# Gathered token rows staged through DRAM and turned on VectorE in the expert part of an attention and mixture-of-experts kernel

## The reference, cut to what matters

```
x = layernorm(x + attention(x))                  # 16 x 1024 tokens of 256 features
logits = x @ wr.T; idx = top 2 of 8 experts      # gate = softmax over the two
xg = x[dispatch]                                 # rows of each expert's tokens, at most 5120
h  = gelu(xg @ w1[e] + b1[e])                    # 256 -> 1024
y  = h @ w2[e] + b2[e]                           # 1024 -> 256
out = sum over the two experts of gate * y
x = layernorm(x + out)
```

## Time and profile before

| what | value |
|---|---|
| time of the runs | 2178.67 us median, 2173.41 to 2183.92 |
| span of the profiled execution, first to last instruction | 2074.6 us |
| the median less the span | 104.1 us |
| PE busy | 2003.8 us, 97% |
| DVE busy | 1457.5 us, 70% |
| ACT busy | 1230.1 us, 59% |
| POOL busy | 1249.4 us, 60% |
| mean granted TensorE clock | 0.990 of full speed |
| DMA moved | 173.30 MB, 84 GB/s |

### The profile page before, as it was taken

How to read it: one execution, slowest core, us unless ns; L and a number is a source line. 1 busy time by engine, 2 the same in 40 slices (tenths; PEclk the granted TensorE clock), 3 DMA queues, 4 the chain that set the end, 5 groups by cost and what they waited for, 6 DMA issues and landing times.

```text
span 2074.6 us, 51556 instructions
## 1 busy us (share of the span) xinstructions
PE 2003.8 (97%) x16208; PEld 1949.7 (94%) x16209; DVE 1457.5 (70%) x4361; ACT 1230.1 (59%) x2770; POOL 1249.4 (60%) x1321
## 2 busy tenths in 40 slices
PE   7999999999889999999999999999999999999996
PEld 6988888988879999999999999999999999999996
DVE  3787877878767686667668666766776676666665
ACT  3566666666645565655556566556565656565563
POOL 1277776776766655656556565556555565655564
PEclk9999999999989999999999999999999999999998
DMA  5244443442232121112112111131132122221221
GB/s 191 84 133 137 139 132 125 148 134 93 83 131 82 48 73 57 51 42 96 51 51 93 56 53 56 56 100 55 60 101 64 56 67 64 67 64 62 69 69 51
DMA packets 102242, 173.30 MB, mean 84 GB/s; under 512 B 26179, under 2 KB 70430, under 8 KB 102064
## 3 DMA queue, kind: packets, MB, share of 16 engines
q0 software_dynamic: 45104, 84.59, 13.4%
q1 hardware_dynamic: 57088, 88.18, 12.7%
HBM read 120.52 MB, written 68.97 MB: 91 GB/s over the span
## 4 chain that ended last, share of the span: by engine, by line
PE 57%; issue 5%; POOL 4%; DMA 4%; DVE 2%; ACT 1%; DVEq 1%; POOLq 0%; ACTq 0%; SPq 0%
PE y_ps L1732 29%; PE h_ps L1716 26%; DMA rows<-x_rows,pick_idx 3%; PE tb_ps L1696 2%; POOL slot_table L461 1%; POOL rows L1407 1%; DMA out<-y,put_idx 1%; POOL base L1420 1%; ACT h_ps L1531 0%; POOL rstd_b L1413 0%; POOL out L1431 0%; DVE y_raw L1578 0%; DVE y L1611 0%; DMA table_in<-slot_table 0%; DVE h_lo L1643 0%
## 5 line engine op out<-in xcount | busy, mean ns | idle before, releaser
L1531 ACT ACTIVATE h_ps<-h_ps,b_sb 128x256 f32<-128x256 f32 x1000 | 403.8, 445 | 566.7 <-PE h_ps L1716 566.7
L1732 PE MATMUL y_ps<-w_hi,h_hi 128*128 128x256 f32 x2000 | 568.1, 284 | 1.8 <-DVE h_lo L1643 1.8
L1716 PE MATMUL h_ps<-bt_hi,w_hi 128*128 128x256 f32 x2000 | 554.8, 277 | 3.0 <-DVE bt_lo L1560 1.5
L1732 PE MATMUL y_ps<-w_hi,h_lo 128*128 128x256 f32 x2000 | 557.0, 278 | 0.0
L1732 PE MATMUL y_ps<-w_lo,h_hi 128*128 128x256 f32 x2000 | 556.4, 278 | 0.0
L1716 PE MATMUL h_ps<-bt_lo,w_hi 128*128 128x256 f32 x2000 | 553.5, 277 | 0.0
L1716 PE MATMUL h_ps<-bt_hi,w_lo 128*128 128x256 f32 x2000 | 553.4, 277 | 0.0
L1716 PEld LDWEIGHTS h_ps<-bt_hi,w_hi 128*128 128x128 f32 x2000 | 376.3, 188 | 4.7 <-issue 2.7
L1732 PEld LDWEIGHTS y_ps<-w_hi,h_hi 128*128 128x128 f32 x2000 | 377.3, 189 | 3.3 <-DVE h_lo L1643 3.1
L1643 DVE TENSOR_TENSOR h_lo<-h_ps,h_hi 128x512 fp32r<-128x512 f32 x500 | 332.3, 682 | 64.1 <-ACT h_hi L1534 63.9
L1732 PEld LDWEIGHTS y_ps<-w_hi,h_lo 128*128 128x128 f32 x2000 | 376.5, 188 | 0.0
(11 more groups left out here) (281 smaller groups left out, 3615.6 us busy)
## 6 DMA issues: line engine op xcount, KB each, us to landing
xt_raw<-in_x_t SPq DMA_DIRECT2D x32, 512.0 KB
x_raw<-in_x SPq DMA_DIRECT2D x64, 256.0 KB, 3.3
w_raw<-in_w SPq DMA_DIRECT2D x16, 1024.0 KB
x_rows<-x_sb SPq DMA_DIRECT2D x32, 512.0 KB, 3.9
out<-alone SPq DMA_DIRECT2D x32, 512.0 KB, 4.5
slot_table<-entry,where POOLq DMA_INDIRECT x256
out<-y,put_idx POOLq DMA_INDIRECT x253
rows<-x_rows,pick_idx POOLq DMA_INDIRECT x250
```

The lines of the kernel that those rows point to most:

```text
L1531: nc.scalar.activation(half, half, ACT.Gelu_apprx_tanh, bias=b1_sb[:, bass.ds(e * FT + 2 * g + i, 1)]).then_inc(gelu_done, 1)
L1716: ins = nc.tensor.matmul(h_ps[:, g, (f % 2) * BLK:(f % 2 + 1) * BLK], w[:, c:c + P], v[:, k, :], start=(i == 0), stop=(i == 3 * DK - 1))
L1732: ins = nc.tensor.matmul(y_ps[:, t, :], v[:, g, h:h + P], w[:, c:c + D], start=(f == 0 and t == 0 and part == 0), stop=(f == FT - 1 and t ...
```

## The change

A block's rows no longer go from the gather to PE. SP stores the gathered tile to a DRAM buffer `stage` (`store_rows`) and loads it back in four DMAs (`load_x4`), one for each band of 64 features, so that each 32 partitions of `x4` hold one band of 32 tokens at a time. DVE turns the 32x32 pieces with one transpose (`turn_rows`, L1603 of the changed kernel) into the SBUF tile `turned`, from which ACT and DVE make `bt_hi` and `bt_lo`. Feature d then lies on partition d // 2, so the weights `w1` are loaded as "(p k) f", and the transposes that remain on PE (the first block and the four small ones) read every second feature. ACT's two copies go: SP loads `base` from `stage` (`load_base`). The gather runs one block further ahead, gather(n + 2) in body n; the tile `rows` is free again when its store has landed (`stored`), and `pick` moves to the head of DVE's body. Block 1's rows are gathered before the expert part begins, into `rows_second`. The loads of the next expert's weights and of `b2` move from SP to ACT.

```diff
+    stage_dram = nc.dram_tensor("stage", ((E * BLOCKS + 2) * BLK, D), F, kind="Internal").ap()
+        rows_second = keep("rows_second", [P, BT, D])
+        def interleaved(row, k):
+            return row.rearrange("p (i k) -> p k i", k=DK)[:, k, :]
             sp.dma_start(w_raw[:, 0:W1].rearrange("p (k f) -> p k f", k=DK),
-                         w1[e, :, :].rearrange("(k p) f -> p k f", p=P)).then_inc(w_loaded, 16)
+                         w1[e, :, :].rearrange("(p k) f -> p k f", p=P)).then_inc(w_loaded, 16)
...
-                for t in range(BT):
-                    pool.indirect_dma_start(
-                        out=rows[:, t, :], out_offset=None, in_=x1_dram,
-                        in_offset=bass.IndirectOffsetOnAxis(ap=table_in[:, t, 0:1], axis=0)).then_inc(gathered, 16)
+                for block, dst, landed in ((0, rows, first_gathered), (1, rows_second, gathered)):
+                    for t in range(BT):
+                        pool.indirect_dma_start(
+                            out=dst[:, t, :], out_offset=None, in_=x1_dram,
+                            in_offset=bass.IndirectOffsetOnAxis(ap=table_in[:, block * BT + t, 0:1], axis=0)).then_inc(landed, 16)
...
-            x1_next = sb("x1_next", [P, BT, D])
+            x4 = sb("x4", [P, BLK // 32, D // 4])
+            turned = sb("turned", [P, 2 * BLK])
...
+                def store_rows(n, src, done):
+                    sp.dma_start(block_of(n).rearrange("(t p) d -> p t d", p=P), src[:, :, :]).then_inc(done, 16)
+                def load_x4(n):
+                    sp.wait_ge(stored, 16 * n)
+                    by_band = block_of(n).rearrange("(g j) (c e) -> c j g e", j=32, c=4)
+                    for c in range(4):
+                        sp.dma_start(x4[c * 32:(c + 1) * 32, :, :], by_band[c]).then_inc(x4_loaded, 16)
+                def load_base(n):
+                    sp.wait_ge(sum_step, STEPS * n + 1)
+                    sp.dma_start(base[:, :, :], block_of(n).rearrange("(t p) d -> p t d", p=P)).then_inc(base_done, 16)
...
                 sp.wait_ge(attention_left, ENGINES)
-                sp.dma_start(b2_sb[:, :], b2.rearrange("(a e) d -> a (e d)", a=1).broadcast_to([P, E * D])).then_inc(b2_loaded, 16)
-                with sp.Fori(0, E - 1) as e:
-                    sp.wait_ge(w_split, 2 + 8 * 2 * e)
-                    load_expert(sp, e + 1)
+                sp.wait_ge(first_gathered, 16 * BT)
+                store_rows(0, rows, first_stored)
+                sp.wait_ge(gathered, 16 * BT)
+                store_rows(1, rows_second, stored)
+                load_x4(1)
+                sp.wait_ge(first_stored, 16)
                 total = all_blocks(sp)
+                with sp.Fori(0, total) as n:
+                    load_base(n)
+                    sp.wait_ge(gathered, 16 * BT * (n + 2))
+                    store_rows(n + 2, rows, stored)
+                    wait_apart(sp, xt_ready, n + 1)
+                    load_x4(n + 2)
+                sp.wait_ge(x4_loaded, 64 * (total + 1))
                 wait_apart(sp, put_done, 16 * BT * (total + 1) + 16)
...
-                def gather(n, unit=None):
-                    pool.wait_ge(next_done, n)
-                    if unit is not None:
-                        wait_apart(pool, h_used, (n - 2) * UNITS + unit)
-                    wait_apart(pool, pick_ready, n)
+                def gather(n):
+                    pool.wait_ge(stored, 16 * (n - 1))
+                    wait_apart(pool, pick_ready, n - 1)
-                    pool.wait_ge(base_done, n + 1)
+                    pool.wait_ge(base_done, 16 * (n + 1))
+                pool.wait_ge(first_stored, 16)
...
-                    gather(n + 1)
+                    gather(n + 2)
...
-                    gather(n + 1, 3)
+                    gather(n + 2)
...
-                def split_hi(n):
-                    act.wait_ge(xt_ready, n + 1)
-                    nc.scalar.activation(xt_hi[:, :, :].rearrange("p k n -> p (k n)"), t_ps[:, :], ACT.Copy).then_inc(bt_hi_done, 1)
-                def lay_base(n):
-                    act.wait_ge(sum_step, STEPS * n + 1)
-                    act.wait_ge(next_done, n + 1)
-                    nc.scalar.activation(base[:, :, :], x1_next[:, :, :], ACT.Copy).then_inc(base_done, 1)
-                def keep_rows(n):
-                    if not (isinstance(n, int) and n == 0):
-                        act.wait_ge(base_done, n)
-                    act.wait_ge(gathered, 16 * BT * (n + 1))
-                    nc.scalar.activation(x1_next[:, :, :], rows[:, :, :], ACT.Copy).then_inc(next_done, 1)
+                def split_hi(src=turned):
+                    nc.scalar.activation(xt_hi[:, :, :].rearrange("p k n -> p (k n)"), src[:, :], ACT.Copy).then_inc(bt_hi_done, 1)
                 act.wait_ge(attention_left, ENGINES)
-                split_hi(0)
-                keep_rows(0)
+                act.wait_ge(first_turned, 1)
+                split_hi(t_ps)
+                act.dma_start(b2_sb[:, :], b2.rearrange("(a e) d -> a (e d)", a=1).broadcast_to([P, E * D])).then_inc(b2_loaded, 16)
+                load_expert(act, 1)
...
-                        if g == late_base:
-                            lay_base(n)
-                    split_hi(n + 1)
-                    keep_rows(n + 1)
+                        if load and g == 1:
+                            act.wait_ge(w_split, 2 + 16 * (e + 1))
+                            load_expert(act, e + 2)
+                    act.wait_ge(xt_ready, n + 1)
+                    split_hi()
...
+                    with act.Fori(5, blocks) as block:
+                        body(before + block, e, eu)
...
-                def split_lo(n):
+                def split_lo(n, src=turned):
                     dve.wait_ge(bt_hi_done, n + 1)
-                    V.tensor_tensor(xt_lo[:, :, :].rearrange("p k n -> p (k n)"), t_ps[:, :],
+                    V.tensor_tensor(xt_lo[:, :, :].rearrange("p k n -> p (k n)"), src[:, :],
                                     xt_hi[:, :, :].rearrange("p k n -> p (k n)").bitcast(F), ALU.subtract).then_inc(bt_lo_done, 1)
                 def pick(n):
+                    dve.wait_ge(gathered, 16 * BT * (n - 1))
                     V.tensor_copy(pick_idx[:, :], column(n + 1, 0)).then_inc(pick_ready, 1)
+                def turn_rows(n):
+                    dve.wait_ge(x4_loaded, 64 * n)
+                    V.transpose(turned[:, :].rearrange("p (b g i) -> p b g i", b=DK, i=32),
+                                x4[:, :, :].rearrange("p g (i b) -> p b g i", b=DK)).then_inc(xt_ready, 1)
...
-                split_lo(0)
+                split_lo(0, t_ps)
                 dve.wait_ge(table_padded, 4)
-                pick(1)
                 gates(0)
...
+                    if e == 0 and turn == 3:
+                        dve.wait_ge(table_padded, 4 + 1)
+                    pick(n + 2)
...
+                        if g == UNITS - 2:
+                            turn_rows(n + 1)
...
-                            pick(n + 2)
...
-                def transpose_rows(n):
-                    pe.wait_ge(gathered, 16 * BT * (n + 1))
-                    for k in range(DK):
-                        for t in range(BT):
-                            c = k * BLK + t * P
-                            ins = nc.tensor.transpose(t_ps[:, c:c + P], rows[:, t, k * P:(k + 1) * P], ident[:, :])
-                    ins.then_inc(xt_ready, 1)
                 pe.wait_ge(attention_left, ENGINES)
-                transpose_rows(0)
+                pe.wait_ge(first_gathered, 16 * BT)
+                for k in range(DK):
+                    for t in range(BT):
+                        c = k * BLK + t * P
+                        ins = nc.tensor.transpose(t_ps[:, c:c + P], interleaved(rows[:, t, :], k), ident[:, :])
+                ins.then_inc(first_turned, 1)
...
-                    transpose_rows(n + 1)
```

28 lines of the change are left out of this document (17 added, 11 removed).

## The result

The changed kernel takes 2237.53 us (median of 4 runs, 2229.82 to 2238.43), the kernel before 2181.3 on the same chip: ratio 1.026, 95% interval 1.0226 to 1.0293. The sign was forecast; the size, +17 us, was not: it is +56. The record does not name this chip, and the changed kernel was timed on no other, so wherever a later run's ratio is set against 1.026, two chips may be compared.

The account below looks back on a forecast made before the run. The prediction took PE's own instructions to bound the kernel. Plain blocks +14.6, changes of expert +7, the last change -3.4 and start -1 gave +17 us: 2092 span plus 104.1 around it, 2196 us, range 2150 to 2238.

Parts of the forecast that it names:

- The bound: Plain blocks: nothing but PE's own instructions sets the step, 11.39 us (11.50 in even experts).
- Pick, gathers, `root`, multiply, `h_lo`: Chain on DVE and POOL from `y_raw`: gather +1.73, `root` +4.03, `h_lo` pair +6.35; PE then waits some 0.56 us a block.
- The rival of an unhindered PE: Plain blocks: `root` not held up by the gathers, PE sets the block at 10.93 us, total 2103; chance 16 in 100.
- The step that failed: Plain block's end: `down(1)` weight load to next `y_raw` takes 4.52 us, so the block takes 11.55, not 11.39.
- A term put at nothing: Load of `base` from DRAM: there about 2.5 us after the add, while POOL is still at its gathers, so no cost.
- The gain: Four transposes taken off PE in each block but the first: 0.44 to 0.47 us a block.
- Changes of expert: Six blocks around each change: about +1.15 us each, six times, +7 us in all; range 0 to +20.
- the last one: The last change of expert: rows come a block earlier, -3.4 us (-4 to -2).
- Start: Start of the expert part: two more gathers, but first rows there earlier; -1 us, between -5 and +5.
- Nothing for the stores and loads: SP's stores and loads through DRAM: landing covered in time, the store's by 2.4 us, so no cost.
- Longer gathers beside the add: POOL's gathers beside DVE's add: 0.27 us longer each, +44 us more, 2240; chance 7 in 100.
- Slow staging: Store to DRAM takes 7.5 us rather than 3.9: 1.2 us more a block, near 2345; chance 7 in 100.

Follow-up runs that it names:

- the second trace: A second profile of the kernel before, without an edit; its span is 2176.0 us, where the trace the prediction used had 2074.6.
- half_put: Changed kernel with one of POOL's two writes of finished rows left out in each block (half the output not written); ratio to the kernel before 1.0025.
- no_x4: Changed kernel without SP's four loads of `x4` in each block; ratio 0.5% lower than the changed kernel's.
- one_row: Changed kernel with `x4` loaded by one DMA in place of four, same bytes, rows in a wrong order; ratio 0.7% lower than the changed kernel's.
- h_lo_first: Changed kernel with DVE's multiply and finish of rows moved behind `h_lo` of the second unit; only 0.8% gained against the changed kernel.
- between_late_put: Changed kernel with POOL's `root` between the two gathers and its second write of finished rows waiting for the block's `y_raw`; ratio to the kernel before 1.0151.
- all_three: Changed kernel with `root` between the gathers, second write behind `y_raw`, second unit's `h_lo` ahead of multiply and finish; 2141.67 us, ratio to the kernel before 0.9894.
- half_put_h_lo_first: Changed kernel with second unit's `h_lo` ahead of multiply and finish, and one of POOL's two writes left out; ratio to the kernel before 0.9756.
- empty_put: Changed kernel whose second write of finished rows has indices beyond the bound, so it is issued but writes nothing; ratio in the band 1.02 to 1.03.
- root_first: Changed kernel with POOL's `root` ahead of both gathers rather than behind them; 2318.55 us.
- one_row_root: Changed kernel with one load of `x4` in place of four and `root` ahead of both gathers; its forecast of about 2120 us fell by 170 us.

## Why the prediction was right in sign and wrong in size

- **The bound.** Right: PE's own instructions, in every trace. The sum's base was wrong. It laid 104.1 us around the span; the second trace has them inside, as a longer attention part and blocks with gaps. Its own range was also added up 2 to 3 us too narrow: the ends of its four terms, -5 and +55, give 2174 to 2234, not 2176 to 2231.
- **Pick, gathers, `root`, multiply, `h_lo`.** Right to 0.1 us: +1.73, +4.03, +4.80, +6.35 forecast; +1.71, +4.04, +4.82, +6.26 in the block above; medians of `root` and the pair +4.03 and +6.25. The rival of an unhindered PE (2103) fell, as PE waits 84 times and 81.4 us.
- **The step that failed** is the line "from the weight load of `down(1)` to the next `y_raw` is 4.52: 11.51, with a few hundredths 11.55". It takes over from before that `y_raw` follows PE's last matmul as closely as it did. The edit made the block longer for POOL, whose wait for `base` and four issues end with the second write near PE's last matmul, and `y_raw` fell 0.30 us back (median). As the whole chain hangs on `y_raw`, PE's extra step at `down(1)` is 0.87 in the mean of plain blocks, not 0.56. With the lag gone, in half_put, the plain block is 0.22 above before: the forecast's +0.18 was near for the chain alone.
- **A term put at nothing stands ahead of it.** The prediction had `base` "about 2.5 us after the add, when POOL is still at its gathers". In the block above SP issues that load at +2.07, the adds end at +1.87, and POOL, done with `root` at +4.79, goes on only at +5.92 (median of plain blocks +5.73, against +4.25 in the second trace of before). By this row the second write would else end up to 1.1 us earlier, where the lag was small in half_put (0.43 in 90 blocks with the issue 1.2 to 2.0 ahead). That is an estimate: no run takes this wait away alone.
- **The gain was over-sized.** Before, the place of the transposes costs 0.37 over an ordinary step (mean of 79 blocks), not 0.44 to 0.47: the slower matmul behind them (0.09) is there in the changed kernel too (0.11). So a plain block changes by 0.87 - 0.37 = +0.50 at `down(1)`, 0.02 behind it, 0.08 where `down(0)` waits, 0.03 in the pace: +0.63 of the measured +0.64, where +0.18 was forecast. Times 79 that is 50 us: the lag is about 24 of the missing 36, the gain 7, the gaps the rest.
- **Changes of expert and the last one.** +2.3 for +7, inside its range; -1.7 for -3.4, just outside (-4 to -2). Start: +4.1 for -1, inside.
- **Nothing for the stores and loads.** Their landing was covered, as said (a store lands in 2.2 us), but the load of `base` was not. Whether the loads of `x4` cost anything stays open: no_x4 and one_row are lower by 0.5 and 0.7%, within touching intervals.
- **Longer gathers beside the add.** Wrong rival: 993 ns a gather, 1013 in the second trace of before. But the gathers do not lie beside the add, as the prediction took it: in the block above the first overlaps the adds (+0.99 to +1.87) by 0.16 us, the second not at all. So the rule of the Trainium skill (SBUF — State Buffer, "SBUF: two separate sides"), a port pair that a DVE operation with two SBUF inputs locks against GpSimd, was hardly tried here.
- **Slow staging.** Wrong for the store, for which POOL waited 6 times, 21 us; what POOL waited for in most blocks was the load of `base`.

Shown: PE's wait for `h_lo` and the lag of `y_raw` together are the loss, since with all rows written each remedy alone gives back little (h_lo_first 0.8%, between_late_put 1.1%) and all_three 3.7%; without the second write it is 2.3% for half_put and 5% for half_put_h_lo_first. Shown: taking the second write away or moving it takes the median lag away, on two chips (half_put and between_late_put; half_put_h_lo_first and, in half of its blocks, all_three); on a third, and in the changed kernel's trace, the lag only goes with the place of the write. Not shown: what holds the wake-up and PE, the issue or its transfers; why the kernel before bears the same place 0.5 to 1.0 us behind; why the first write's issue at nearly the same place does nothing in between_late_put; why one chip has none of it. On that chip the changed kernel itself was not run, so it may cost less there.

## What to carry to other kernels

Work taken off the busiest engine pays only as far as the next chain allows, and that chain can be followed to a tenth of a microsecond from rows; but check also where each DMA issue of the other engines comes to lie against the wake-ups that the chain starts with. Taking work out from between two ends of the chain (`h_lo` ahead of the multiply) removed PE's wait wholly, 0.00 left at `down(1)`, where reordering POOL with `root` between the gathers left 0.54; neither paid much until the second write was moved too. A copy that a DMA takes over is a wait to be placed as well: here POOL's 1.1 us for `base`. Before a sum is made against a profile's span, see that the span is that of the timed runs.

## What the runs showed of the hardware

- `y_raw` on DVE starts 0.43 us after the start of PE's last matmul in the kernel before (median, both traces). In the changed kernel it is 0.74 where the issue of POOL's second write ended 0.25 to 0.5 us ahead of that matmul (43 blocks) and 0.89 where it ended 0 to 0.25 ahead (23). Such an issue does not do it everywhere: 0.43 in between_late_put for the first write (18 blocks) and in empty_put (49). In root_first it took up to 3.2, and in one_row_root PE itself took a matmul each 0.7 us.
- The same kernel takes 2078 us on one chip and 2161 to 2177 on three others. The granted clock is 1.00 from 700 to 1900 us in both traces of it, and 0.99 and 0.96 in the first 600 us; 64 of the 101 us between the traces lie in the attention part, the rest are gaps and late wake-ups in the expert part.
- SP's load of 256 KB from DRAM into `base` let POOL go on 3.85 us after its issue (1315.82 to 1319.67), where a store of the same size landed in 2.2.
- A 128x512 transpose by DVE takes 0.70 us, and SP needs 2.27 us for four loads of 64 KB, whether in pieces of 256 or 2048 bytes.
